# Scores to values with a longer lag, a float32 projection, reciprocals spread within SBUF, and the convolution's output ahead of the projection's on the vector engine

## What is computed

```python
x = x + _L0_conv_ref(_gn(x), qkv_weight, qkv_bias, proj_weight, proj_bias, rel_pos_table)
x = x + _L1_conv_ref(_gn(x), w, pruning_mask)
...
# _L0: windows of 7 x 7 of the image shifted by 3, 8 heads of 16 channels
q = q * hd ** (-0.5)
attn = jnp.einsum('whnd,whmd->whnm', q, k) + rpb + mask
attn = jax.nn.softmax(attn, axis=-1)
x = jnp.einsum('whnm,whmd->whnd', attn, v)
x = x @ proj_weight.T + proj_bias
# _L1: 3 x 3 convolution, 128 to 128 channels, weights magnitude-aware sign + pruning mask
```

## Time and profile before

| | us |
|---|---|
| three runs of the kernel | 3644.57, 3646.91, 3647.12 |
| median | 3646.91 |
| the profiled execution | 3636.98 |
| span in its trace | 3635.2 |
| mean granted clock of PE | 0.983 |

### The profile page before, as it was taken

How to read it: one execution, slowest core, us unless ns; L and a number is a source line. 1 busy time by engine, 2 the same in 40 slices (tenths; PEclk the granted TensorE clock), 3 DMA queues, 4 the chain that set the end, 5 groups by cost and what they waited for, 6 DMA issues and landing times.

```text
span 3635.2 us, 155064 instructions
## 1 busy us (share of the span) xinstructions
PE 3190.5 (88%) x64395; PEld 2684.8 (74%) x64395; DVE 3073.1 (85%) x6399; ACT 2555.1 (70%) x5729; POOL 2365.1 (65%) x3683
## 2 busy tenths in 40 slices
PE   2889989889899899898899999889898899898896
PEld 1667777777777777777777777777777777787775
DVE  5689888888888888888888888888888898888895
ACT  1667777767677777777777777777677777777772
POOL 4466666766667666667766667766667666667763
PEclk9999999999999999999999999999999999999998
DMA  2111111111111111111111111111111111111111
GB/s 57 37 42 52 47 42 47 49 50 49 37 47 50 49 52 47 42 47 50 52 52 50 42 45 49 50 52 50 37 47 50 50 52 47 42 47 50 34 35 36
DMA packets 260489, 169.26 MB, mean 47 GB/s; under 512 B 23120, under 2 KB 259792, under 8 KB 259792
## 3 DMA queue, kind: packets, MB, share of 16 engines
...
## 4 chain that ended last, share of the span: by engine, by line
PE 33%; DVE 32%; issue 13%; POOL 9%; DMA 8%; ACT 4%; SPq 0%; DVEq 0%; ACTq 0%; POOLq 0%
PE conv_ps L1014 8%; DVE s_sb L766 6%; PE qkv_ps L895 6%; DMA recip_wide<-recip_dram 5%; PE attn_ps L932 4%; PE scores_ps L908 4%; PE attn_ps L936 4%; DVE plane_lo L778 3%; POOL s_sb L443 3%; DVE s_max L771 3%; DMA recip_dram<-recip 3%; DVE oT_lo L759 3%; PE probsT_ps L919 3%; DVE tok_lo L856 3%; DVE recip L746 2%
## 5 line engine op out<-in xcount | busy, mean ns | idle before, releaser
L443 POOL TENSOR_TENSOR s_sb<-s_sb,s_max 113x392 f32<-113x392 f32 x1024 | 998.9, 975 | 1092.7 <-DVE s_max L771 1091.4
L505 ACT COPY probsT<-probsT_ps 128x392 f32<-128x392 f32 x1024 | 490.8, 479 | 376.6 <-PE probsT_ps L919 366.4
L498 ACT ACTIVATE probs<-s_sb 113x392 f32<-113x392 f32 x1024 | 552.4, 539 | 221.1 <-POOL s_sb L443 218.6
L470 POOL TENSOR_TENSOR plane<-x_n 128x224 f32<-128x224 f32 x896 | 656.4, 753 | 18.7
L919 PE MATMUL probsT_ps<-ident,probs 113*128 113x113 f32 x4096 | 585.0, 265 | 38.7 <-ACT probsT L505 35.3
L771 DVE TENSOR_REDUCE s_max<-s_sb 113x8 f32<-113x392 f32 x1024 | 574.9, 561 | 35.3
L766 DVE TENSOR_TENSOR s_sb<-scores_ps,bias 113x392 f32<-113x392 f32 x1024 | 565.8, 552 | 41.0 <-PE scores_ps L908 37.1
L569 ACT COPY v<-qkv_ps 64x256 f32<-64x256 f32 (+2 forms) x1280 | 391.0, 325 | 211.6 <-PE qkv_ps L895 205.5
L1014 PE MATMUL conv_ps<-plane_hi,wc_hi 128*128 128x224 f16 x2688 | 484.4, 263 | 23.1 <-DVE conv_y L840 19.0
L919 PEld LDWEIGHTS probsT_ps<-ident,probs 113*128 113x128 f32 x4096 | 433.5, 141 | 90.7 <-ACT probs L498 47.9
L908 PE MATMUL scores_ps<-k,q 32*49 32x98 f32 x16384 | 477.4, 252 | 19.7 <-issue 19.4
...
## 6 DMA issues: line engine op xcount, KB each, us to landing
x_in<-in_x_dram SPq DMA_DIRECT2D x224, 224.0 KB, 3.9
recip_wide<-recip_dram SPq DMA_DIRECT2D x256, 196.0 KB
out_dram<-x_out SPq DMA_DIRECT2D x224, 224.0 KB, 2.3
recip_dram<-recip SPq DMA_DIRECT2D x256, 12.2 KB, 1.7
...
```

The source lines that it names most:

```text
L443: nc.gpsimd.tensor_tensor(s, s, top, ALU.subtract).then_inc(sub_ready, 1)
L470: last = nc.gpsimd.tensor_tensor(plane[:, t % 2, j], *sums[j])
L498: nc.scalar.activation(probs[0:QP, slot % 2, :, :, 0:N], s_sb[0:QP, slot % 4], ACT.Exp)\
L505: nc.scalar.copy(probsT[:, g % PT_SLOTS], probsT_ps[:].rearrange("p (w n) -> p w n", n=ODD)[:, :, 0:N])\
```

## The change

Seven edits, all in one version.

1. The probabilities are turned 3 units after the scores (`LAG_T`), with three `probs` buffers; the values of a row come at units 7, 11, ... and inside the unit ahead of `qkv`; what follows moves with them (`RECIP_AT` 8, `NORMED_AT` 10, `PROJ_AT` 11).
2. v is made for the current row, q and k for the next one. New functions number the products, since at the two ends of an image some are left out.
3. The reciprocals go from SBUF to SBUF in four DMAs of 128 pieces of 392 bytes, without the way through DRAM.
4. DVE's reciprocal and multiplication come behind the bias and maximum of their unit.
5. `oT_hi` and `oT_lo` are gone: the projection is one float32 product of `o_sb` and `w_proj`.
6. DVE combines the convolution's sums ahead of the projection's addition to the image. The convolution starts at unit 16; its 36 matmuls are issued in three units in place of four.
7. The second norm's matmuls, its first use on POOL and the turns of the next image's input move by a unit or two.

```diff
-LAG_T = 2
-VALUES_AT, NORMED_AT, SPLIT_AT = 5, 8, 9
+LAG_T = 3
+PROBS = 3
+VALUES_AT, RECIP_AT, NORMED_AT = 7, 8, 10
-PROJ_AT = 9
-G2_JOBS = ((6, END), (7, MID))
-NORM2_AT = 9
-VHI_AT, VLO_AT = 10, 12
-TIN_JOBS = ((10, END), (12, END), (14, MID), (14, END), (15, MID), (17, MID), (18, END))
+PROJ_AT = 11
+G2_JOBS = ((8, END), (9, MID))
+NORM2_AT = 10
+VHI_AT, VLO_AT = 11, 13
+TIN_JOBS = ((9, END), (10, END), (13, MID), (13, END), (14, END), (17, MID), (17, END))
-CONV_AT, CONV_STEPS = 12, 4
+CONV_AT, CONV_STEPS = 16, 4
-CONV_PARTS = ((0, 2, 4), (3, 4, 5), (2, 2, 2), (6, 6, 0))
+CONV_PARTS = ((0, 6, 6), (5, 5, 4), (4, 3, 3), (0, 0, 0))
...
+def qkv_job(i, u):
+    r, j = divmod(u, PAIRS)
+    if j < 2:
+        return live(i, 0 if r < ROWS - 1 else 1)
+    return live(i) or (i, u) == (-1, UNITS - 1)
...
         # SP
-                        sp.dma_start(recip_dram[row % 2].rearrange("h (a n) -> (h a) n", a=SUM_PARTS),
-                                     recip[0:128:4, :]).then_inc(recip_out, 16)
                         need(sp, o_ready, row)
-                        sp.wait_ge(recip_out, 16 * (row + 1))
-                        sp.dma_start(recip_wide[:], bass.AP(tensor=slot.tensor, offset=slot.offset,
-                                                            ap=[[RT, HEADS], [0, HD], [1, RT]]))\
-                            .then_inc(recip_wide_in, 16)
+                        for a in range(SUM_PARTS):
+                            sp.dma_start(recip_wide[:, a * SUM_COLS:(a + 1) * SUM_COLS],
+                                         recip[SUM_PARTS * a:128:HD, :].unsqueeze(1).to_broadcast((HEADS, HD, SUM_COLS)))\
+                                .then_inc(recip_wide_in, 16)
...
         # ACT
-                need(act, probsT_ready, g - 1)
-                nc.scalar.activation(probs[0:QP, slot % 2, :, :, 0:N], s_sb[0:QP, slot % 4], ACT.Exp)\
+                need(act, probsT_ready, g - PROBS + 1)
+                nc.scalar.activation(probs[0:QP, g % PROBS, :, :, 0:N], s_sb[0:QP, slot % 4], ACT.Exp)\
-                        nc.scalar.copy(flat(oT_hi), flat(o_sb)).then_inc(oT_hi_ready, 1)
...
         # DVE
-                        vec.tensor_tensor(flat(oT_lo), flat(o_sb), flat(oT_hi), ALU.subtract).then_inc(oT_lo_ready, 1)
...
         # PE
-                    pe.wait_ge(oT_lo_ready, i * ROWS + (t + 1 if u >= PROJ_AT else t + 1 - ROWS))
-                    hi, lo = (o[:].rearrange("p r w -> p (r w)") for o in (oT_hi, oT_lo))
-                    last = three(misc_ps[:, 0:RT], ((wT_hi[:, 3, :], hi), (wT_hi[:, 3, :], lo), (wT_lo[:, 3, :], hi)))
+                    pe.wait_ge(o_ready, i * ROWS + (t + 1 if u >= PROJ_AT else t + 1 - ROWS))
+                    last = mm(misc_ps[:, 0:RT], w_proj[:], flat(o_sb), start=True, stop=True)
...
                     conv(i, u, 1)
-
-                    if live(i, 0 if u // PAIRS < ROWS - 1 else 1):
+                    row = row_of(i, u, VALUES_AT)
+                    if row is not None:
+                        values(row)
+                    if qkv_job(i, u):
                         qkv(i, u)
                     conv(i, u, 2)
                     for job in misc_at(i, u, (END,)):
                         misc(i, u, *job)
-                    row = row_of(i, u, VALUES_AT)
-                    if row is not None:
-                        values(row)
```

150 lines of the change are left out of this document (76 added, 74 removed).

## The result

The changed kernel takes 3683.40 us (median of 4 runs, 3677.57 to 3688.30), the kernel before on the same chip 3645.74: ratio 1.0111, interval 1.0083 to 1.0138. It is 1.1% slower where 4.2% faster was forecast, and outside the range. The profiled execution's span is 3680.7 us, its mean granted clock 0.958 (0.983 before).

A forecast was written before the change was run, and what follows sets the result against it. The bound was taken to change within an image: PE, DVE, or waits for POOL's norm chains. Terms summed to -153 us, 3636.98 to 3484, or 3494 us on the 3646.91 base (4.2% less); range 3390 to 3640.

The forecast's parts named there:

- Second norm, third row: POOL's chain with first norming and two planes between two subtractions: PE's wait grows, 29 us lost, ends 0 and 67.
- First norm, seventh row: More PE work ahead of its stop for POOL's chain covers 2.4 of 3.17 us: 77 us gained, ends 0 and 101.
- Convolution: The convolution's waits for `plane_lo` vanish with three units between: 35 us gained, ends 0 and 35.
- `oT_lo` off DVE, and ACT's rounding: Fourth, fifth, sixth, eighth row: DVE freed, 75 us gained, ends 0 and 224; ACT's rounding counted as nothing.
- Float32 product: Projection on PE steps by 0.79 us instead of 0.59, in six rows of eight: 38 us lost, ends 0 and 105.
- Half clock: Seventh row, partly at 1.2 GHz after PE's wait: a shorter wait gains 0.5 us an image, 16 us.
- Reciprocals: Four DMAs on SP's queue, two units from reciprocal to multiplication as now: neither lost nor gained.
- The end: Last image: three more halves of planes ahead of DVE's first convolution sum, 6 us lost, ends 0 and 12.
- The rival of late reciprocals: The four DMAs do not overlap, so DVE and PE stand in every row: 294 us lost, 3788 us, chance 0.11.
- PE binds at once: Rival: no row shorter than PE's busy time over 0.965; 58 us less, 3589 us, chance 0.15.
- the signs of being wrong: PE waits for `o_sb` or DVE's image addition; DVE's reciprocal wait far above 103; fifth, sixth, eighth row unshortened, PE at 97%.

The follow-up runs named there:

- e11: The kernel before with only the projection as one float32 product of the unsplit attention output: 3531.25 us, ratio 0.9705 to the kernel before.
- e17: The kernel before with two parts of the change, the float32 projection and the reciprocals from SBUF to SBUF: 3520.33 us, ratio 0.9675.
- e18: The kernel before with float32 projection, reciprocals from SBUF to SBUF, and the convolution starting at unit 16 instead of 12: 3523.74 us, ratio 0.9681.
- e3: The changed kernel with the second norming, all planes and the first norming one unit later: 3608.21 us, ratio 0.9897 to the kernel before.
- e7: The changed kernel with one Newton step in place of three for both norms, a less exact result: 3482.18 us, ratio 0.9572.
- e20: e17 with the second norm's last small product one unit later, so chain, first norming and two planes fall between two POOL subtractions: 3574.69 us, ratio 0.9815.
- e4: The changed kernel with the projection as three 16-bit passes over one 16-bit attention output, low half left out: 3651.74 us, ratio 1.0018.
- e1: The changed kernel with 36 extra unread matmuls per image on PE in units 13 to 15: 3680.14 us, ratio 1.0093 to the kernel before.
- e12: The changed kernel with the reciprocals carried through DRAM in two DMAs as before: 3830.57 us, ratio 1.0537 to the kernel before.
- e22: e3 with the second norm's two small products and the first tile's turn moved later, within or around unit 9: 3586.10 us, ratio 0.9870.

## Why the prediction was wrong

By parts, forecast and measured: the projection with what it frees, -75 - 23 + 38 = -60 against -109 (e11); the reciprocals 0 against -11 (e17 less e11, not told apart from nothing); the moves in time, -77 + 29 - 35 - 16 + 6 = -93 against +163 (3683.40 less e17's 3520.33). The last figure is a remainder, so the three add up (to +43, with e11's own kernel before as the base) whatever the reasons are; only the first two were measured by themselves.

*Second norm, third row: the step that failed.* I had seen that the first norming and two planes would come between the chain's two subtractions, priced that at 2.1 us, set 1.2 us of PE's work against it and wrote 29. That counts one stop of PE. But POOL does not catch up for 15 us; every subtraction in that time is late, and the turns, scores and bias additions of four units follow POOL. The forecast put the loss into the third row; it came in the fourth, behind the stop. The third and fourth row are together 4.9 us an image longer than in e18, 157 over the run, and 3.8 of the 4.9 lie in the fourth. Parting the stack takes 3.1 us an image off the fourth row again, 75 off the run (e3), a shorter chain 3.3 (e7); making the stack on e17 costs 54 (e20). The upper end of 67 was too low as well. The third row keeps its 13.5 in e3 and in e7; what makes it 1.2 longer than in e18 stays open.

*First norm, seventh row.* 77 was forecast. The row became 0.8 us an image shorter, 26, and the projection alone does as much (15.68 in e11); against e17 it is 0.3, 11 over the run. The stop moved from the values to the turn, as I had it, but the change also puts POOL's last plane pair, unit 23, between that chain and the norming: 8.2 us from subtraction to subtraction on average, 7.1 before. I did not count that pair.

*Convolution.* The wait for `plane_lo` went, but not by the later convolution: it is gone in e17 already, for a gain of some 11 that isn't told apart from nothing, and moving the convolution then brought nothing (e18). 35 was too many.

*`oT_lo` off DVE, and ACT's rounding.* Under-sized: with the dearer product at +32 (e4, on the changed kernel), what is freed is worth some 141 by estimate, where I had 75 + 23. Nor is it where I put it: in e11 the fourth and fifth row gain 0.1 and 0.2, the sixth and eighth 0.8 and 0.7, and the first, third and seventh, which I had left out, 0.6, 0.6 and 0.85. ACT's part I put at nothing because it is nowhere above 81%; in the eighth row it is at 83%. No run parts ACT's share from DVE's.

*Float32 product.* Right: 0.81 a step where I took 0.79, and 32 where I took 38.

*Half clock.* I forecast a gain of 16. The time at half clock rose from 125 to 309 us of the span, most of the rise in the fourth row (5.5 us an image, 0.2 before); in the seventh, for which the gain was forecast, it went from 2.7 to 3.1. By e1 it costs little by itself: the fourth row became 0.5 shorter without it, with 3.5 us of matmuls added.

*Reciprocals.* Nothing lost, as forecast, but that was luck. I took the time from reciprocal to multiplication as unchanged; it fell from a median of 5.8 to 4.6 us, and only the shorter way, 4.2 at the least where the one by DRAM took 5.0, fits into that. With the way by DRAM the rest of the change costs 147 more (e12). The rival of late reciprocals fell: DVE's wait went down from 103.0 to 73.2. The Trainium skill's page DMA: Bandwidth & Descriptors (Why small descriptors are slow), which limits the penalty for small pieces to HBM, is in line with that; no run here tells it from a penalty too small to be seen.

*The end.* From the last image's first bias addition to the end of the span are 186.6 us, 172.9 before: 13.7 more, where I had 6 and at most 12.

*The rivals.* "PE binds at once" was right for the first and second row (11.71 and 13.24, for its 11.9 and 13.2), where PE is at 100% of the row, and wrong for the total. No rival had POOL as the engine that becomes the bound, though the earlier trace rows had it at 92% in the fourth row; the first took POOL's 12.7 there as it was. Nor did the signs of being wrong name it: they are waits of PE and DVE, and rows with PE at 97%.

Open: e3 gives back 75 of the 163, e22 some 10 to 22 more. DVE's order was not tried alone, nor the later projection, the values inside the unit, or v made for the current row. The sixth row is 1.0 longer than in e17, with DVE at 97% in both. In one image's sixth row `plane_lo` takes 819 ns on average, 668 in e17, and `gn_var` 730, 497 in e17. The Trainium skill's page SBUF — State Buffer (Who interferes with whom) has a DVE operation with two inputs in SBUF, as `plane_lo` has, contend with GpSimd's reads. The trace fits: of the 448 `plane_lo` of the changed kernel 300 last over 0.7 us, and POOL is busy beside these nearly all along; before they were 52. But no run took the contention away.
